# A mixture-of-experts layer on one core: a tile's row additions wait for the preceding tile only where their token ranges meet

## The reference, cut to what matters

```python
h = einsum('bct,bcd->bdt', x, cond_weights[itok])          # 128 x 32 x 256
scores = sigmoid(h @ gate_w.T);  sb = scores + gate_bias   # 4096 x 32
group_scores = top_k(sb.reshape(T, 4, 8), 2)[0].sum(-1)
_, gidx = top_k(group_scores, 2)                           # 2 of 4 groups
...
y_lat = sum over chosen experts of cw * relu2((h @ fc1_w.T) @ w1[e].T) @ w2[e].T
routed = y_lat @ fc2_w.T
shared = relu2(h @ shared_up_w.T) @ shared_down_w.T
return x + shared + routed
```

## Time and profile before

| | |
|---|---|
| median of 3 runs | 437.25 us (436.96 to 437.43) |
| the profiled execution | 437.96 us |
| its span, first to last instruction | 436.2 us |
| PE busy | 383.4 us (88%), mean granted clock 0.963 |
| DVE, ACT, POOL busy | 307.4, 253.5, 200.5 us |
| additions (POOL, L530) | 70, first at 194.5 us, last at 428.9 us |

### The profile page before, as it was taken

How to read it: one execution, slowest core, us unless ns; L and a number is a source line. 1 busy time by engine, 2 the same in 40 slices (tenths; PEclk the granted TensorE clock), 3 DMA queues, 4 the chain that set the end, 5 groups by cost and what they waited for, 6 DMA issues and landing times. The chain is left out here.

```text
span 436.2 us, 6956 instructions
## 1 busy us (share of the span) xinstructions
PE 383.4 (88%) x2224; PEld 332.0 (76%) x2224; DVE 307.4 (70%) x581; ACT 253.5 (58%) x330; POOL 200.5 (46%) x153
## 2 busy tenths in 40 slices
PE   8798989998799667999999999999999999998520
PEld 8787988998689565788888888888888888888410
DVE  0258999999998514788778778778787787875300
ACT  1364445555365503677777877778777778775300
POOL 5000076857777400014544467563564345533561
PEclk9999999999999969899999999999999999999955
DMA  6992573942943788768988998999998899989542
GB/s 172 252 294 68 191 256 104 303 137 83 347 140 117 243 235 251 228 199 197 227 223 218 217 216 219 225 239 340 345 324 231 219 223 321 349 214 259 81 41 31
DMA packets 66249, 93.55 MB, mean 214 GB/s; under 512 B 19295, under 2 KB 48086, under 8 KB 65622
## 3 DMA queue, kind: packets, MB, share of 16 engines
q1 hardware_dynamic: 52210, 77.71, 55.6%
q0 software_dynamic: 13296, 15.08, 20.6%
q10 hardware_dynamic: 708, 0.32, 0.3%
HBM read 94.48 MB, written 30.18 MB: 286 GB/s over the span
## 5 line engine op out<-in xcount | busy, mean ns | idle before, releaser
L530 POOL DMA_INDIRECT out_x<-res,sid_sb x70 | 123.2, 1759 | 159.6 <-DMA out_x<-res,sid_sb 71.6
L1011 DVE TENSOR_TENSOR act_lo<-act_full,act_hi 128x1024 fp32r<-128x1024 f32 (+3 forms) x92 | 106.0, 1152 | 25.3 <-ACT act_full L874 21.0
L1274 DVE SCALAR_TENSOR_TENSOR scaled<-h_banks,cond_bd 128x1024 f32<-128x1024 f32 (+3 forms) x76 | 86.5, 1138 | 40.2 <-PE h_banks L694 39.9
L694 PE MATMUL h_banks<-xc_hi,w_ring 128*128 128x512 f32 (+3 forms) x304 | 95.2, 396 | 3.0 <-issue 0.8
L509 POOL DMA_INDIRECT rows_dram<-payload,slot_idx x64 | 70.2, 1097 | 47.9 <-DVE payload L1149 25.3
L715 PE MATMUL y_banks<-act_hi,w_ring 128*128 128x512 f32 (+3 forms) x304 | 78.0, 379 | 5.6 <-ACT act_hi L872 5.6
L872 ACT ACTIVATE act_hi<-scaled 128x1024 fp32r<-128x1024 f32 (+3 forms) x76 | 75.0, 986 | 2.6 <-PE y_banks L715 1.7
L874 ACT ACTIVATE act_full<-scaled 128x1024 f32<-128x1024 f32 (+3 forms) x76 | 74.7, 983 | 0.0
L715 PEld LDWEIGHTS y_banks<-act_hi,w_ring 128*128 128x128 f32 x304 | 55.5, 190 | 16.7 <-ACT act_hi L872 5.2
L694 PEld LDWEIGHTS h_banks<-xc_hi,w_ring 128*128 128x128 f32 x304 | 51.6, 191 | 15.0 <-issue 6.0
L694 PE MATMUL h_banks<-xc_lo,w_ring 128*128 128x512 f32 (+3 forms) x152 | 57.8, 380 | 0.0
(11 more groups left out here) (147 smaller groups left out, 617.4 us busy)
## 6 DMA issues: line engine op xcount, KB each, us to landing
w_ring<-w_dram SPq DMA_DIRECT2D x76, 512.0 KB
cond_bd<-s_dram SPq DMA_DIRECT2D x64, 512.0 KB, 5.5
w_dram<-w_ring SPq DMA_DIRECT2D x8, 1024.0 KB, 7.0
x_in<-in_x SPq DMA_DIRECT2D x8, 512.0 KB, 6.6
res<-in_experts_raw SPq DMA_DIRECT2D x4, 1024.0 KB, 10.6
out_x<-x_in SPq DMA_DIRECT2D x8, 512.0 KB, 3.7
rows_sb<-rows_dram SPq DMA_DIRECT2D x16, 256.0 KB, 5.3
rows_dram<-in_pad_rows SPq DMA_DIRECT2D x5, 328.0 KB, 4.4
```

Of the source, the lines that this page charges most:

```text
L530: pool.indirect_dma_start(out, bass.IndirectOffsetOnAxis(ap=sid_sb[:, i % SID_RING, j, GROUP_SIZE:PER_GROUP], axis=0), res[:, i % 2, j * H ...
L694: last = pe.matmul(h_banks[:, s, m * BANK:m * BANK + SIZE[i]], w, v, start=n == 0, stop=n == 2)
L1011: dve.tensor_tensor(lo, full, hi.bitcast(f32), ALU.subtract).then_inc(act_lo_ready, 1)
L1274: dve.scalar_tensor_tensor(pair(scaled, i, u), h, 0.0, scale, ALU.max, ALU.mult).then_inc(scaled_ready, 1)
```

## The change

The tiles' additions count on two semaphores, `out_added[0]` for even and `out_added[1]` for odd tiles; `ADDS_BY[i]` is the number of additions of tile i and of those of its parity ahead of it. Everybody who waited for the additions of a certain tile waits on the semaphore of its parity. POOL reads the first and the last token id of each tile into registers (`read_ids`, two loads from `sid_sb` per tile). From tile 3 on, it waits for tile i-2 always, and for tile i-1 to a count that it works out in registers: with tile i-1's additions where the two ranges of ids meet, without them (as far as tile i-3) where they don't. Behind this wait it adds one to `tokens_apart`, on which nobody waits.

```diff
-ADDS_TO = [sum(ROWS_OF[:n]) for n in range(X_TILES + 1)]
+ADDS_BY = [sum(ROWS_OF[n % 2:n + 1:2]) for n in range(X_TILES)]
+ID_BITS = 13
...
-        out_added = sem("out_added")
+        out_added = sems("out_added", 2)
+
+        tokens_apart = sem("tokens_apart")
...
-                    sp.wait_ge(out_added, ADDS_TO[i - SID_RING + 1] * DMA)
+                    sp.wait_ge(out_added[i % 2], ADDS_BY[i - SID_RING] * DMA)
...
-            sp.wait_ge(out_added, ADDS_TO[X_TILES] * DMA)
+            for i in range(X_TILES - 2, X_TILES):
+                sp.wait_ge(out_added[i % 2], ADDS_BY[i] * DMA)
...
+            lowest, highest = [], []
+
+            def read_ids(i):
+                ids_of = sid_sb[:, i % SID_RING, :, GROUP_SIZE:PER_GROUP]
+                lowest.append(pool.value_load(ids_of[0:1, 0, :], min_val=0, max_val=TOKENS + BANK - 1))
+                highest.append(pool.value_load(ids_of[P - 1:P, ROWS_OF[i] - 1, :], min_val=0, max_val=TOKENS + BANK - 1))
+
+            def wait_for_shared_tokens(i):
+
+                reaches = (highest[i - 1] - lowest[i] + (1 << ID_BITS)) >> ID_BITS
+                starts = (highest[i] - lowest[i - 1] + (1 << ID_BITS)) >> ID_BITS
+                meets = (reaches & starts) & 1
+                pool.wait_ge(out_added[(i - 1) % 2], (ADDS_BY[i - 3] + meets * ROWS_OF[i - 1]) * DMA)
+                pool.sem_inc(tokens_apart, 1)
+
             for i in range(X_TILES):
                 pool.wait_ge(sid_loaded[i % SID_RING], (i // SID_RING + 1) * DMA)
-                if i > 0:
-
-                    pool.wait_ge(out_added, ADDS_TO[i] * DMA)
+                read_ids(i)
+                if i >= 2:
+                    pool.wait_ge(out_added[i % 2], ADDS_BY[i - 2] * DMA)
+                if i >= 3:
+                    wait_for_shared_tokens(i)
+                elif i > 0:
+                    pool.wait_ge(out_added[(i - 1) % 2], ADDS_BY[i - 1] * DMA)
...
-                        res[:, i % 2, j * H:(j + 1) * H], None, compute_op=ALU.add).then_inc(out_added, DMA)
+                        res[:, i % 2, j * H:(j + 1) * H], None, compute_op=ALU.add).then_inc(out_added[i % 2], DMA)
...
-                    act.wait_ge(out_added, ADDS_TO[i - 1] * DMA)
+                    act.wait_ge(out_added[i % 2], ADDS_BY[i - 2] * DMA)
```

## The result

| | before | after |
|---|---|---|
| median | 437.11 us (436.69 to 437.43, 4 runs) | 431.31 us (430.90 to 432.46, 4 runs) |
| profiled execution, its span | 437.96 us, 436.2 us | 430.90 us, 429.1 us |

The ratio is 0.9872, with a 95% interval of 0.9851 to 0.9893: 5.8 us gained where 8.1 were forecast. The time lies inside the stated range (425.8 to 433.0 us).

The account below looks back on a forecast made before the run. PE bounds the kernel until the tail, then the chain of additions from tile 15: span 436.2 - 11.3 (earlier last addition) + 2.7 (slower landing) + 0.5 (handovers) = 428.1 us, 429.1 us against the median; range 425.8 to 433.0 us.

Parts of the forecast that it names:

- The bound: PE bounds the kernel from 194 to 390 us; late additions cost only in the tail, as one chain from tile 15.
- PE's stretch from 194 to 390 us: PE, busy 194.57 of 196 us there before the change, was to stay unchanged.
- Which tiles meet: Id ranges computed from the inputs: tiles 4, 5, 10, 12, 13, 16, 17 and 18 meet their predecessor; 14 and 15 don't.
- Rival (c): Counts or ranges in registers keep the wait for tiles 14 and 15; only 0.5 us added, 437.5 us; chance 0.06.
- The wait goes for tiles 14 and 15: POOL's wait for the preceding tile goes at tiles 14 and 15, stays at 16, 17 and 18; PE hides earlier ones.
- Tile 15's last addition: On POOL, it starts at 398.3 us instead of 409.62 us, 11.3 us earlier.
- Its landing: Landing of tile 15's last addition: taken as 6.5 us against 3.8 in the tail, giving back 2.7 us.
- the bound of 8.6 us: Upper limit for the landing of tile 15's last addition, the longest seen before 404 us.
- Handovers: Steps to tiles 16, 17 and 18: 0.15 us more each behind the wait, 0.5 us in all; loads hidden.
- Rival (d): Id loads dear on POOL, paid three times beyond 3.0 us per tile; 443.6 us at 4 us each; chance 0.04.
- The sum: Profiled span 436.2 - 11.3 + 2.7 + 0.5 = 428.1 us; against the median 437.25 - 8.1 = 429.1 us.
- Rival (b): Tile 14's and 15's additions queue on loaded DMA engines: last landing about 409 us, gain 4.4 us, 432.9 us; chance 0.06.

Follow-up runs that it names:

- skip_to_13: The changed kernel, but tiles 14 and 15 wait for the tile ahead as before the change, so only tiles up to 13 are freed: 432.96 us, ratio 0.9892.
- wait_to_13: The changed kernel, but tiles 1 to 13 wait for all additions ahead as before; the range decides only from tile 14 on: 431.67 us, ratio 0.9888.
- no_pad_weights: The changed kernel, but the 2 MB of weights named for the all-padding tile 18 are not loaded: 428.87 us, ratio 0.9806.
- loads_x4: The changed kernel with each tile's two id loads made four times over, eight loads: 434.84 us, ratio 0.9893.

## Why the prediction was right, point by point

**The bound.** Right: PE binds until tile 15's data, then the additions' chain. The freed waits removed ACT's waits of 3.84, 5.42 and 5.49 us, and with all waits kept the gain was gone (1.0032). PE's stretch from 194 to 390 us was to stay unchanged and did not: it lost 1.6 us.

**Which tiles meet.** Right for the time: the list as constants gives 0.9870, the registers 0.9872 and 0.9925, and in the trace the tiles on the list wait for a landing while tile 14 does not. Rival (c) is out.

**"The wait goes for tiles 14 and 15 ... (Further ahead 4, 5, 10 and 12 meet their predecessor; PE hides all of those.)"** Half right. Freeing 14 and 15 alone suffices (0.9888), but so does freeing the earlier ones alone (0.9892). The forecast took the backlog as given at tile 14. In the trace of before it comes in steps. A tile's first addition starts 2.1 to 3.6 us behind the end of its first copy for tiles 1 to 7, 4.9 to 6.9 us for tiles 8 to 13, 8.3 us for tile 14 and 12.6 us for tile 15. Tiles 7 and 8, first copy and first addition:

```profile
286.35 0.60 ACT L908 ACTIVATE res<-t_banks 128x512 f32<-128x512 f32 x1 [0.99 <-PE t_banks L733]
...
299.69 0.60 ACT L908 ACTIVATE res<-t_banks 128x512 f32<-128x512 f32 x1 [1.00 <-PE t_banks L733]
```

```profile
289.28 2.59 POOL L530 DMA_INDIRECT out_x<-res,sid_sb  x1 [3.87 <-DMA out_x<-res,sid_sb]
...
305.17 1.55 POOL L530 DMA_INDIRECT out_x<-res,sid_sb  x1 [6.42 <-DMA out_x<-res,sid_sb]
```

With the early tiles alone freed, it is 4.2 us at tile 13, 4.7 at tile 14 and 5.4 at tile 15 (skip_to_13). Free links in either group keep it small.

**Tile 15's last addition.** 398.3 us forecast, 399.14 measured: 10.5 us earlier than before, not 11.3. The missing 0.8 us are PE's delay by its waits for weights, 1.9 us, less a start that came 1.0 us earlier (tile 0's copy at 192.06 instead of 193.10 us); the forecast held PE's stretch to be fixed, and it scatters.

**Its landing.** The mis-sized term. Taken as 6.5 us, measured 7.7: 1.2 us. The argument that the weights end a few microseconds after 398 us was no reason for a shorter landing: SP started the last load of the padding tile's weights at 400.92 us, the DMA engines' share stayed between 0.84 and 1.19 until 406 us, nearly as long as the landing lasted (to 406.8 us), and without these weights it is 5.7 us. In other profiles the landing came near or above the bound of 8.6 us (8.4 and 8.9 us in the two of wait_to_13), so the bound was too tight.

**Handovers.** 0.5 us forecast for three; nothing shows at the two that can be compared: 8.22 us from tile 16 to 17 and 6.37 us from 17 to 18, against 8.29 and 6.39 us before. A load takes 0.47 or 0.48 us on POOL (medians), between SP's 0.27 and its longest, 1.30. Rival (d) needed loads of 5.9 us a tile; eight of them, some 6 us, exposed 1.5 us at tile 18, nothing at tile 17 and about 1.8 us at tile 15. It was right only in that loads beyond their cover are paid, and wrong on the cover.

**The sum.** In the span: 0.8 + 1.2 us more, 0.5 us less for the handovers, and 0.5 us less at the end (422.20 to 429.1 us against 428.85 to 436.2): 428.1 forecast, 429.1 measured. That the span came so close is in part luck: half of 2.0 us of errors was cancelled by others. The other 1.2 us of the 2.2 on the median come from the step from one execution to the median: the forecast took the changed kernel's profiled execution to lie 0.7 us above its median, as before's did, and it lay 0.4 us below.

**Rival (b),** queueing of the eight additions: it had tile 15's last landing at about 409 us, and it came at 406.8 us. The eight are the same in no_pad_weights, where the landing fell to 5.7 us, so 2.0 of the 3.9 us above the tail's landing went with the weights; for the other 1.9 us queueing is not excluded. In full the waits did not come back: the last addition came 10.5 us earlier, and its landing took 3.9 us more than before.

## What to carry to other kernels

A serial chain of transfers that falls behind the engine beside it shows no cost until the engine stops: measure how late each link starts behind its data, and the lateness of the last one is what can be won. Here some free links, early or late, were enough to win it; what is left afterwards is the last landing, so look at what streams beside it, here weights that nobody needed. And a kernel that has lost its backlog passes its engine's chance delays on to the last addition, where a backlog can swallow them (3.6 us in one profile here).

## What the runs showed of the hardware that was not expected

POOL's register loads of an id took 0.47 or 0.48 us each (medians), SP's of the table 0.27 and 0.28, and POOL's ran while its queued indirect transfers were still being prepared: in loads_x4 eight loads hid between tile 16's first addition and tile 17's. The landing of one 128-row addition was 7.7 us beside the stream of the padding tile's weights, 5.7 us without it, and 3.7 to 3.9 us in the tail of before, where the DMA engines' share was 0.38.
